# Two convolutions on one core: another order of the second one's products, with the 32x64 rounds of three products joined in one run

## The reference, cut to what matters

```python
x = x + _L0_conv_ref(_gn(x), w3, b3, w5, b5, wr, br)   # x: (8, 32, 64, 64)
x = x + _L1_conv_ref(_gn(x), filters)

# _L1_conv_ref: 3x3 patches, a one in front, all products of two entries
spot = jnp.concatenate([ones, _extract_patches(x, 3, 1, 1)], axis=-1)      # 10 entries
feat = (spot[..., :, None] * spot[..., None, :]).reshape(... + (100,))
out = jnp.einsum('bcyxf,ocf->boyx', feat, filters.reshape(O, C, 100))
```

## Time and profile before

| | |
|---|---|
| time, median of three executions | 303.23 us (300.46 to 304.02) |
| span of the profiled execution | 300.4 us |
| the execution next to it in time | 300.46 us |
| PE busy | 273.3 us (91%) |
| DVE busy | 252.8 us (84%) |
| ACT busy | 87.6 us (29%) |
| share of TensorE in the chain that ended last | 71% |

### The profile page before, as it was taken

One profiled execution on the slowest core, in us unless ns is written; L12 is line 12 of the kernel. 1 busy time (PEld: TensorE's weight loads), 2 busy tenths in 40 slices (PEclk: granted clock), 3 DMA queues, 4 the chain that ended last, 5 costly groups with the idle time before them and its releaser, 6 DMA issues.

```text
span 300.4 us, 13567 instructions
## 1 busy us (share of the span) xinstructions
PE 273.3 (91%) x6464; PEld 130.6 (43%) x6464; DVE 252.8 (84%) x216; ACT 87.6 (29%) x135; POOL 29.0 (10%) x82
## 2 busy tenths in 40 slices
PE   0589999899999999999999999999999999999930
PEld 0224343344434433363546475344345446467310
DVE  1899899998999979799999999984999999970330
ACT  4532006979169789539000000004000000000000
POOL 7913920000110000000000000000000000000000
PEclk9999999999999999999999999999999999999995
DMA  6973000000000000000000000085000000000049
GB/s 190 382 203 82 4 2 3 2 5 2 2 2 4 4 2 4 2 2 3 4 2 4 2 4 4 2 171 115 2 2 4 2 2 4 2 4 4 2 91 189
DMA packets 19206, 11.45 MB, mean 38 GB/s; under 512 B 17744, under 2 KB 17872, under 8 KB 19024
## 3 DMA queue, kind: packets, MB, share of 16 engines
q1 hardware_dynamic: 14640, 9.06, 11.9%
q10 hardware_dynamic: 4512, 1.53, 2.2%
HBM read 6.40 MB, written 4.19 MB: 35 GB/s over the span
## 4 chain that ended last, share of the span: by engine, by line
PE 71%; DVE 15%; ACT 4%; issue 3%; DMA 2%; SPq 1%; DVEq 0%
PE acc L1007 63%; PE acc L1050 7%; ACT raw L507 3%; DMA raw<-in_x 2%; DVE stats L741 2%; DVE product L637 2%; DVE plane L759 2%; PE acc L1101 2%; DVE scaled L637 1%; DVE raw L801 1%; DVE product L872 1%; DVE product L663 1%; DVE product L669 1%; DVE arena L669 1%; DVE product L673 1%
## 5 line engine op out<-in xcount | busy, mean ns | idle before, releaser
L1007 PE MATMUL acc<-product,weight 32*32 32x512 f32 (+1 forms) x3072 | 126.8, 604 | 0.3 <-DVE product L872 0.3
L1007 PEld LDWEIGHTS acc<-product,weight 32*32 32x32 f32 (+1 forms) x3072 | 65.2, 110 | 59.4 <-issue 41.5
L879 DVE TENSOR_TENSOR product<-plane 128x4096 f32<-128x4096 f32 x19 | 83.3, 4430 | 0.1
L1007 PE MATMUL acc<-raw,weight 32*32 32x512 f32 (+1 forms) x960 | 45.4, 604 | 0.0
L1050 PE MATMUL acc<-product,middle 32*64 32x512 f32 (+1 forms) x576 | 30.2, 598 | 0.0
L1007 PEld LDWEIGHTS acc<-raw,weight 32*32 32x32 f32 (+1 forms) x960 | 20.7, 112 | 20.2 <-issue 15.7
L801 DVE TENSOR_TENSOR raw<-acc,arena 128x512 f32<-128x512 f32 x16 | 9.9, 683 | 16.7 <-issue 16.6
L1007 PE MATMUL acc<-product,arena 32*32 32x512 f32 (+1 forms) x448 | 22.2, 604 | 0.0
L879 DVE TENSOR_TENSOR raw<-plane 128x4096 f32<-128x4096 f32 x5 | 22.1, 4428 | 0.0
L741 DVE BATCH_NORM_STATS2 stats<-raw 128x6 f32<-128x512 f32 x32 | 19.7, 681 | 2.7 <-DMA raw<-in_x 2.6
L507 ACT ACTIVATE raw<-arena 32x512 f32<-32x512 f32 x32 | 21.8, 681 | 0.5
(11 more groups left out here) (121 smaller groups left out, 209.9 us busy)
## 6 DMA issues: line engine op xcount, KB each, us to landing
raw<-in_x SPq DMA_DIRECT2D x8, 512.0 KB, 8.3
out<-raw SPq DMA_DIRECT2D x24, 128.0 KB, 3.0
arena<-in_L_conv_filters SPq DMA_DIRECT2D x4, 400.0 KB, 6.9
out<-raw ACTq DMA_DIRECT2D x8, 128.0 KB, 4.7
arena<-in_L_conv_w ACTq DMA_DIRECT2D x4, 100.0 KB, 4.0
w_in<-in_L_conv_w ACTq DMA_DIRECT2D x2, 36.0 KB, 1.8
w_in<-in_L_conv_w SPq DMA_DIRECT2D x2, 36.0 KB, 2.2
b_in<-in_L_conv_b SPq DMA_DIRECT2D x2, 0.5 KB
```

The lines of the kernel that those rows point to most:

```text
L879: nc.vector.tensor_tensor(both_halves(g, u), plane_halves(g), plane_halves(g, PRODUCTS[k][0] * PITCH + PRODUCTS[k][1]), ALU.mult)\
L1007: return nc.tensor.matmul(acc[32 * s:32 * (s + strips), j, r, :], weights[32 * r:32 * r + 32, t:t + strips, :] .rearrange("p t c -> p (t c ...
```

## The change

The list of offsets ends (1, 0), (2, -1), (2, 0) instead of (2, -1), (2, 0), (1, 0): unit 15 is now the offset (1, 0) with three columns and two rows of taps, unit 16 is (2, -1), and the last unit 17 is (2, 0), with three columns and one row. The weights follow the list by themselves, and so do VectorE's multiplications, whose order, number and size stay. The order on TensorE is now written out: units 7, 8, 9 together with their pairs in one run, units 10, 11, 12 in singles, units 13, 14, 15 together with their pairs in one run, and units 16 and 17 in singles.

```diff
-PRODUCTS = (..., (1, 2), (1, -2), (2, -1), (2, 0), (1, 0))
+PRODUCTS = (..., (1, 2), (1, -2), (1, 0), (2, -1), (2, 0))
...
-                for u in range(7, LAST_UNIT):
-                    wait_made(g, u)
-                    if len(rows_of(PRODUCTS[u - 5])) == 1:
-                        forms = (False,)
-                    else:
-                        forms = (in_pairs, not in_pairs)
-                    for pairs in forms:
-                        taps1(g, 0, u, pairs)
-                        last = taps1(g, 1, u, pairs)
-                    last.then_inc(unit_used, 1)
-                    in_pairs = forms[-1]
+                def both(u, pairs):
+                    taps1(g, 0, u, pairs)
+                    return taps1(g, 1, u, pairs)
+
+                def three(a, b, c):
+
+                    wait_made(g, a)
+                    both(a, SINGLES)
+                    both(a, PAIRS).then_inc(unit_used, 1)
+                    wait_made(g, b)
+                    both(b, PAIRS)
+                    wait_made(g, c)
+                    both(c, PAIRS)
+                    both(b, SINGLES).then_inc(unit_used, 1)
+                    both(c, SINGLES).then_inc(unit_used, 1)
+
+                three(7, 8, 9)
+                for u in (10, 11, 12):
+                    wait_made(g, u)
+                    both(u, SINGLES).then_inc(unit_used, 1)
+                three(13, 14, 15)
+                wait_made(g, 16)
+                both(16, SINGLES).then_inc(unit_used, 1)
                 wait_made(g, LAST_UNIT)
-                taps1(g, 0, LAST_UNIT, in_pairs)
-                taps1(g, 0, LAST_UNIT, not in_pairs, True).then_inc(half_done, 1)
-                taps1(g, 1, LAST_UNIT, not in_pairs)
-                taps1(g, 1, LAST_UNIT, in_pairs, True).then_inc(half_done, 1)
+                taps1(g, 0, LAST_UNIT, SINGLES, True).then_inc(half_done, 1)
+                taps1(g, 1, LAST_UNIT, SINGLES, True).then_inc(half_done, 1)
```

More of the change, by code:

```diff
@@ L49 @@
 N_WEIGHT0 = CORNER_AT + len(CORNERS)
-PRODUCTS = ((0, 0), (0, 1), (1, 1), (1, -1), (0, 2), (2, 2), (2, -2), (2, 1), (1, 2), (1, -2), (2, -1), (2, 0), (1, 0))
+PRODUCTS = ((0, 0), (0, 1), (1, 1), (1, -1), (0, 2), (2, 2), (2, -2), (2, 1), (1, 2), (1, -2), (1, 0), (2, -1), (2, 0))
 N_PRODUCTS = len(PRODUCTS)
@@ L1232, in _ @@
                     taps1(g, 1, NEXT, SINGLES).then_inc(unit_used, 1)
-                    in_pairs = False
                 else:
```

## The result

The changed kernel takes 303.62 us (median of 20 executions, 301.77 to 306.58), the kernel before, measured beside it, 302.94 (20 executions). The ratio is **1.0034, 95% interval 1.0019 to 1.0050**: 1.0 us slower (0.6 to 1.5), well inside 2%. The forecast was +1.1 us and 304.3.

The account below looks back on a forecast made before the run. TensorE's matmul sequence was taken to bound the kernel; +1.74 (group 0), +0.05 (change of groups) and -0.70 (group 1) gave +1.1 us on the median 303.23, so 304.3; range 301.6 to 305.1, with rivals 300.3 to 305.8.

Parts of the forecast that it names:

- Unit 15 is needed sooner in group 0: Group 0: TensorE wants unit 15 at 167.8 us and stands still until 170.26, a wait of 2.4 us.
- What a run costs: TensorE: one pair of runs (pairs and singles) that disappears is worth 0.35 us, between 0.30 and 0.45.
- The dearer price of 1.2: Rival, TensorE's changes of form: each pair of runs removed gives 1.2 us, for 301.7 us in all; chance 0.06.
- Group 1: Group 1: unit 15 is ready with 1.9 us of cover, so both joined runs count, -0.70 us.
- Group 0's sum: Group 0 on TensorE: +1.74 us, from a wait of 2.4 and joined runs worth -0.7.
- The change of groups: Between groups: the cover of `NEXT` shrinks from 2.5 us to nothing; 0 to 0.5 us, taken as 0.05.
- a wait at `NEXT` of more than 0.5: Sign at the start of group 1: TensorE waiting over 0.5 us for `NEXT` would show the forecast wrong.
- VectorE becomes the bound at the change of groups: Rival between groups: `evict(0, 0)` and `NEXT` set group 1's start, 304.8 to 305.3 us; chance 0.12.
- VectorE's wait for unit 15's buffer: VectorE's square sums of group 1 wait about 1.2 us for unit 15's buffer, with 3 us of cover.
- the rival with the lower level: Rival: TensorE's clock falls in group 0's new wait, 12 rounds cost 5.2 us more, about 309.5 us; chance 0.03.
- No wait in group 0: Rival in group 0: unit 15 causes no wait and all four joins count, -1.4, 301.8 us; chance 0.08.

Follow-up runs that it names:

- late mixing: The changed kernel with VectorE's mixing of group 0's kept halves moved from behind unit 10 to behind unit 15: 300.86 us, ratio 0.9939 to the kernel before.
- the first alone: The kernel before with the pairs of units 7, 8 and 9 in one run in both groups, everything else as before: 301.72 us, ratio 0.9966.
- the second alone: The changed kernel with units 7, 8 and 9 in the old order, the rest as changed: 304.45 us, ratio 1.0046 to the kernel before.

## Why the prediction was right, point by point

- **Unit 15 is needed sooner in group 0.** Right in mechanism, place and size. The wait forecast was 2.4 us, restart 0.07 behind the unit; the unit was made 4.45 us after 166.43, and the loads came at 170.92. The late mixing removes 2.55 us with it, and the same edit in the kernel before removes nothing. That the first join is lost in group 0 is shown by the kernels with one join each: -0.40 with the first alone, and 0.41 between the changed kernel and the second alone, one group's worth both times.
- **What a run costs.** 0.35 us for a pair of runs, with 0.30 to 0.45 as bounds: nine more changes of form cost 1.75 (0.39 a pair), the first join gives 0.42 in group 1. The dearer price of 1.2 (a rival with 0.06) is refuted: for nine changes it would be 5.4 us, and the times give 1.4 to 2.7.
- **Group 1.** The step "both joins count: 2 x 0.35" was too small: -1.13 against -0.70. The first join is 0.42 (by the kernel with it alone), the second then 0.71; the kernel with the second alone gives 0.65 for it and leaves 0.48 for the first. This is the term that was mis-sized. The second join makes one run of 36 rounds of singles out of runs of 30 and 6. With 0.54 a round and 0.15 for the run I had 19.59 us and the bounds 19.4 to 19.9; in group 0 the run took 19.24 (176.38 to 195.62), in the late mixing 19.22 (172.52 to 191.74), so it lies below my lower bound. It isn't that the rounds of a long run are cheaper: the run of 32 rounds takes 17.46 us in group 0 (147.44 to 164.90) and 17.45 in group 1 (243.68 to 261.13), where 0.54 and 0.15 give 17.43. Inside the 36 rounds the first loads of the 31st and the 35th come 15.41 and 17.55 us after the start, at the same pace as in the shorter runs (15.48 for the 31st in the run of 32). The 0.35 us are in the last two rounds with the change behind them, 1.69 us against 2.03 to 2.06 in the runs of 20 and 30 and 1.97 in that of 32. Why they are shorter there is open.
- **Group 0's sum.** Forecast +1.74, measured +1.49; the difference is the same shorter end of the run of 36 (0.35), less 0.07 by which it started late.
- **The change of groups.** I counted 0.05 with a bound of 0.5; it is 0.57, just beyond the bound, so a sign that I had named as wrong (a wait at `NEXT` of more than 0.5) did come. It is the rival "VectorE becomes the bound at the change of groups" (0.12) in its lower part: the chain of waits goes over VectorE's first eviction and `NEXT`, and reading `NEXT` later gains 0.48. Its condition, a half done after 192.4, was just missed (192.91 less the 0.60 of the late start is 192.31). The step that was off is the lag of 0.37 us between the six rounds of a half and its eviction, taken from a half that ended in pairs. In the changed kernel the eviction starts 1.08 us behind the first matmul of the next half (191.83 to 192.91; in group 1 1.06), so VectorE began 2.71 us ahead of the next group (192.91 to 195.62) where I had 3.37 (191.93 to 195.30). The effect on the sum was hidden by the joins being worth 0.43 more: two errors of about half a us with opposite signs.
- **VectorE's wait for unit 15's buffer**, queued ahead of `evict(0, 0)`: forecast about 1.2 us and harmless; 1.35, and 3.09 us of waiting are left behind it. Right.
- **The clock.** In the profiled execution the rival with the lower level did not come: rounds of 0.43 us right behind the longest idle time, and the level in the page is unchanged. But that is one of the thirteen executions with 0.984 to 0.986. The seven with 0.979 to 0.980 have, as an estimate, 0.0055 x 305 = 1.7 us of full clock less and take 0.8 to 3.3 us more than the median of the others. None of the seven was traced, so whether the clock fell in the new wait there is open, and the rival is not refuted for them. For it speaks that the kernel before has 0.982 to 0.988 in all 43 executions timed beside the experiments; against it, that the kernel with the second join alone, whose loads stand idle 2.69 us at the same place, has 0.983 to 0.988 in its twelve. The Trainium skill, "TensorE: Matmul & The Clock Gate", Part 1, has the rule that idleness brings the lower level back; the traces agree at their end, where the last slice, behind the last matmuls, has 0.5, and for the new wait no trace shows a fall.
- **No wait in group 0** (0.08) did not come either.

The near hit of the total, +1.1 against +1.0, is thus better than its parts: +1.74, +0.05 and -0.70 became +1.49, +0.57 and -1.13 in the profile. The +1.0 of the times is in part luck too: against the thirteen executions with the higher clock it is 0.3 to 0.5, with a spread between executions that is larger than that.

## What to carry to other kernels

Before you move the first use of a buffer forward, take the time at which its maker finishes from the trace and compare it with the new time of use; where the maker runs without a gap, everything that is saved ahead of that point is lost in the wait, and a gain must be sought in the maker's order. When an engine's last work on a result gets shorter, count again what it used to cover on the engine that takes over; here moving one step of VectorE and reading one stream later turned 1.0 us of loss into 2.5 us of gain. A gap that the profile shows at a change of mode is no price: compare the lengths of whole runs.

## What the runs showed of the hardware

- A change between 32x32 and 32x64 matmuls shows a gap of 0.84 to 0.88 us between weight loads in place of 0.25, but two of them cost only about 0.4 us net (0.39 with nine changes more, 0.42 to 0.48 with two fewer in group 1).
- A run of 32x32 matmuls takes 0.54 us a round and 0.15 for the run, from 6 to 32 rounds, within 0.15 us where it doesn't wait. The run of 36 rounds at the end of a group takes 19.22 to 19.24 us, 0.35 less, and the difference stands in its last two rounds. The cause is open.
- How late a finished half is handed over is no constant. From the start of its last matmul to VectorE's waiting eviction it took 0.77 to 0.82 us where the half ended in pairs, 0.80 where it ended 14 rounds into a run of singles, and 1.08 to 1.09 where it ended 30 rounds into one. So it isn't the form of the last matmuls alone; the cause is open.
